# Graph attention and expert mixture: layer biases and norm shifts folded into the next projection, expert weights split two experts at a time

## The reference

```python
h = elu(layer_norm(x @ w_in + b_in, g_in, bt_in))
for i in range(3):
    identity = h
    y = gat_conv(h, src, dst, w_l[i], a_s[i], a_d[i], b_l[i])   # p = h @ w_l[i], edge softmax, sum of messages, + b_l[i]
    y = elu(y)
    y = layer_norm(y, g_l[i], bt_l[i])                          # ... * g_l + bt_l
    h = y + identity
...
# experts: softmax gates over 8 experts, three 256 x 256 products for each
h = relu(bn(x @ W1[e] + b1[e])); h = relu(bn(h @ W2[e] + b2[e])); y = h @ Wo[e] + bo[e]; out = sum_e gate_e * y_e
```

## Time and profile before

| | |
|---|---|
| median of three runs | 7070.54 us (7068.94 to 7074.64) |
| the profiled execution | 7087.27 us |
| its span, first to last instruction | 7085.5 us |
| busy: TensorE, VectorE, ScalarE, GpSimd | 5313.8, 4842.8, 4142.8, 3639.1 us |
| the three `gat_finish` stages begin at | 1451.8, 2791.2 and 4117.9 us |
| the expert stage begins at | 4270.4 us |

### The profile page before, as it was taken

How to read it: one execution, slowest core, us unless ns; L and a number is a source line. 1 busy time by engine, 2 the same in 40 slices (tenths; PEclk the granted TensorE clock), 3 DMA queues, 4 the chain that set the end, 5 groups by cost and what they waited for, 6 DMA issues and landing times. The chain is left out here.

```text
span 7085.5 us, 94548 instructions
## 1 busy us (share of the span) xinstructions
PE 5313.8 (75%) x22314; PEld 3799.3 (54%) x22314; DVE 4842.8 (68%) x13222; ACT 4142.8 (58%) x13411; POOL 3639.1 (51%) x3571
## 2 busy tenths in 40 slices
PE   1768888745888886668888616999989787877688
PEld 1645555333555554545555315888874566655346
DVE  5656666694777777767777596666662677778673
ACT  4578888874898988579889762333336322111132
POOL 3477777737777773577777700000000577777201
PEclk8878888876999998779999767999999898887789
DMA  6444444344444443444444332000007534333302
GB/s 184 124 123 116 117 118 117 106 132 139 119 121 122 121 118 104 131 138 124 118 122 118 109 108 65 19 18 27 19 23 267 166 116 128 109 107 101 105 17 74
DMA packets 484001, 763.77 MB, mean 108 GB/s; under 512 B 85543, under 2 KB 360695, under 8 KB 483511
## 3 DMA queue, kind: packets, MB, share of 16 engines
q0 software_dynamic: 166320, 446.82, 22.7%
q1 hardware_dynamic: 317335, 313.36, 13.9%
HBM read 622.82 MB, written 146.27 MB: 109 GB/s over the span
## 5 line engine op out<-in xcount | busy, mean ns | idle before, releaser
L1806 POOL DMA_INDIRECT gm_got<-scratch_feat,keep_src_tab x2490 | 2500.6, 1004 | 776.0 <-issue 669.6
L2028 ACT ACTIVATE gm_got<-gm_got 128x64 f32<-128x64 f32 x9828 | 2393.6, 335 | 5.8 <-DVE gm_got L1941 5.8
L2083 PE MATMUL gm_bank<-gm_got,gm_onehot 128*128 128x264 f32 x4980 | 1783.1, 466 | 385.9 <-DVE gat_acc L1966 229.4
L2083 PEld LDWEIGHTS gm_bank<-gm_got,gm_onehot 128*128 128x128 f32 x4980 | 938.4, 217 | 897.8 <-DVE gat_acc L1966 370.1
L1966 DVE TENSOR_TENSOR gat_acc<-gat_acc,gm_bank 128x264 f32 x2490 | 1059.1, 425 | 498.8 <-PE gm_bank L2083 231.5
L1114 POOL DMA_INDIRECT mix1a_got<-scratch_rel_feat,layer_rel_tab x240 | 240.4, 1002 | 1529.2 <-issue 1528.0
L1114 POOL DMA_INDIRECT mix1b_got<-scratch_rel_feat,layer_rel_tab x590 | 586.9, 995 | 190.5 <-issue 187.2
L1171 PE MATMUL mix1b_m_bank<-mix1b_got,mix1b_onehot 128*128 128x256 f32 x1180 | 379.6, 459 | 153.6 <-DVE layer_acc L1145 132.1
L837 POOL DMA_INDIRECT scratch_first<-gat_scores,keep_first_pos x150 | 216.5, 1444 | 466.9 <-DVE gat_scores L820 425.7
L1973 DVE TENSOR_TENSOR gm_onehot<-keep_iota_row,keep_dst_tab 128x896 f32<-128x896 f32 x357 | 386.5, 1083 | 25.8 <-PE gm_bank L2083 21.9
L1171 PEld LDWEIGHTS mix1b_m_bank<-mix1b_got,mix1b_onehot 128*128 128x128 f32 x1180 | 245.7, 225 | 253.3 <-DVE mix1b_onehot L1123 166.4
(11 more groups left out here) (558 smaller groups left out, 10760.2 us busy)
## 6 DMA issues: line engine op xcount, KB each, us to landing
scratch_rel_feat<-rel_out SPq DMA_DIRECT2D x50, 1024.0 KB, 6.3
gm_got<-scratch_feat,keep_src_tab POOLq DMA_INDIRECT x2490, 2.8
gm_flags<-scratch_flags SPq DMA_DIRECT2D x90, 280.0 KB
gf_feat<-scratch_feat SPq DMA_DIRECT2D x75, 256.0 KB, 4.4
gf_old<-scratch_hidden SPq DMA_DIRECT2D x75, 256.0 KB, 4.7
scratch_hidden<-gf_h SPq DMA_DIRECT2D x75, 256.0 KB, 4.0
scratch_feat<-gf_row SPq DMA_DIRECT2D x50, 260.0 KB, 3.3
gm_x<-scratch_x SPq DMA_DIRECT2D x50, 256.0 KB, 3.1
```

Of the source, the lines that this page charges most:

```text
L1806: nc.gpsimd.indirect_dma_start(out=got[:, place // GROUPS, place % GROUPS * GROUP + j, 0:GAT_ROW], out_offset=None, in_=dram["feat"][layer ...
L2028: last = nc.scalar.activation(rows, rows, ACT.Copy, scale=got[:, b, i, D + h:D + h + 1])
L2083: nc.tensor.matmul(bank[i % BANKS][:, 0:GAT_SUM], onehot[:, i % HOTS, :], got[:, v[1] % B, i, :], start=True, stop=True).then_inc(s_sum, 1)
```

## The change

In the GAT stages the shift `bt_l` is no longer added to the rows. `finish_onto` writes `h = data * rstd + old` in one instruction per tile, instead of `finish` and a sum. What is missing from `h` is a constant row, the sum of the `bt_l` so far. The next projection puts it back: at the start of the stage the constant row is multiplied with `w_l` and added to `b_l` of the coming layer, giving `shift` (its first row filled, the rest zero), and each tile's projection gets one more matmul, of a matrix whose first row alone is ones (`first_row`) with `shift`, accumulated in PSUM. The attention scores get their part from `sc_shift` in the sums that replace two copies. As the attention weights sum to one, `b_l` can go through the projection too, and the sum L2237 goes in layers 1 and 2 (counted from 0; layer 0 keeps it). The expert stage adds the three `bt_l` to its rows.

In the expert stage the first node rows and the weights of experts 0 and 1 are loaded first; the parameters come after; the cutting is done by groups of two experts, the high parts on ScalarE; the rest of the groups is loaded and cut inside the first unit, which stands unrolled ahead of the loop.

```diff
@@ GroupNorm
+    def finish_onto(self, nc, p, out, data, base):
+        u = p % UNROLL
+        nc.vector.wait_ge(self.s_centred, p + 1)
+        for i in range(PAIR):
+            last = nc.vector.scalar_tensor_tensor(out[:, i, :], data[:, i, :], self.rstd[:, u, i:i + 1], base[:, i, :], ALU.mult, ALU.add)
+        return last
@@ Projection.start_sp (layer > 0)
+                for i in range(self.layer):
+                    sp.dma_start(self.c_col[:, i, :], self.io["L0_gnn_bt_l"][i].rearrange("(a p) -> p a", p=P)).then_inc(self.s_c, 16)
+            sp.dma_start(self.b_row[:, :], self.io["L0_gnn_b_l"][self.layer].unsqueeze(0)).then_inc(self.s_c, 16)
@@ Projection.start_dve (layer > 0)
+        nc.vector.memset(self.shift[:, :], 0.0)
+        nc.vector.tensor_copy(self.first_row[:, :], self.ident[:, 0:1].to_broadcast([P, P])).then_inc(self.s_col, 1)
...
+        dve.wait_ge(self.s_line, 1)
+        nc.vector.tensor_tensor(self.shift[0:1, 0:D], self.score_bank[0:1, 0:D], self.b_row[:, :], ALU.add)
+        nc.vector.tensor_copy(self.shift[0:1, D:], self.score_bank[0:1, D:D + 2 * GAT_HEADS]).then_inc(self.s_shift, 1)
+        dve.wait_ge(self.s_spread, 1)
+        nc.vector.tensor_copy(self.sc_shift[:, :], self.score_bank[:, 0:2 * GAT_HEADS]).then_inc(self.s_lined, 1)
@@ Projection.start_pe (layer > 0)
+        for out, rhs in ((self.score_bank[0:1, 0:D], self.w), (self.score_bank[0:1, D:D + S], self.wa)):
+            for k in range(HALVES):
+                last = mm(out, self.c_col[:, 0, k:k + 1], rhs[:, k, :], start=(k == 0), stop=(k == HALVES - 1))
+        last.then_inc(self.s_line, 1)
+        pe.wait_ge(self.s_shift, 1)
+        mm(self.score_bank[:, 0:S], self.first_row[:, :], self.shift[:, D:], start=True, stop=True).then_inc(self.s_spread, 1)
@@ Projection.project_pe
-        project_pair(self.nc, bank, self.ht[:, u], self.w)
+        if self.layer:
+            for i in range(PAIR):
+                out = bank[:, i * D:(i + 1) * D]
+                for k in range(HALVES):
+                    self.nc.tensor.matmul(out, self.ht[:, u, k, i * P:(i + 1) * P], self.w[:, k, :], start=(k == 0), stop=False)
+                self.nc.tensor.matmul(out, self.first_row[:, :], self.shift[:, 0:D], start=False, stop=True)
@@ Projection.scores_dve (layer > 0): two sums with sc_shift in place of two copies
+            self.nc.vector.tensor_tensor(row, sc[:, :, 0:GAT_HEADS], add[:, :, 0:GAT_HEADS].to_broadcast([P, tiles, GAT_HEADS]), ALU.add)
+            self.nc.vector.tensor_tensor(scores, sc, add.to_broadcast([P, tiles, 2 * GAT_HEADS]), ALU.add).then_inc(self.s_sc, size)
@@ gat_finish, vector engine
-                        elif name == "finish":
-                            ln.finish(nc, p, yp, rows["bt_l"]).then_inc(s_ya, 1)
...
-                            nc.vector.tensor_tensor(h[:, u], old[:, p % DEEP], yp, ALU.add).then_inc(s_h, 1)
+                            ln.finish_onto(nc, p, h[:, u], yp, old[:, p % DEEP]).then_inc(s_h, 1)
...
-                        if name == "sums":
+                        if name == "sums" and not layer:
                             dve.wait_ge(s_yf, p + 1)
                             nc.vector.tensor_tensor(yp, yp, both(rows["b_l"][:, :]), ALU.add).then_inc(s_yb, 1)
@@ expert_mixture, sync engine
+                load(sp, 0, slice(0, QUAD))
+                for to, frm in shifts:
+                    sp.dma_start(to, frm).then_inc(s_shift, 16)
+                for j in range(3):
+                    load_weight(j, 0)
                 (the 13 small loads)
-                for j, (to, frm) in enumerate(w_loads):
-                    if j == 2:
-                        sp.wait_ge(s_cutw, 1)
-                    sp.dma_start(to, frm).then_inc(s_wj[j], 16)
-                sp.wait_ge(s_cutw, 2)
-                for s in range(2):
-                    load(sp, s, slice(s * QUAD, (s + 1) * QUAD))
+                for j in range(3):
+                    load_weight(j, 1)
+                load_weight(0, 2)
+                load_weight(1, 2)
+                for j in (1, 2):
+                    sp.wait_ge(s_cutw[j], 2)
+                load(sp, 1, slice(QUAD, 2 * QUAD))
+                load_weight(2, 2)
+                for j in range(3):
+                    load_weight(j, 3)
@@ expert_mixture, front_start
                     c.done(nc.vector.tensor_tensor(x[:, s], x[:, s], h[:, s], ALU.add))
+                    c.done(nc.vector.tensor_tensor(x[:, s], x[:, s], after_gat[:, :].unsqueeze(1).to_broadcast([P, QUAD, D]), ALU.add))
@@ expert_mixture, vector engine
-                for j in range(3):
-                    (wait, high part and low part of a whole tensor)
+                front_start(0, 32)
+                front_statistics(0)
+                front_end(1, 0)
+                cut_weights(0, 0)
                 cut_rows(1)
+                parameters()
+                for j in (1, 2):
+                    cut_weights(j, 0)
+                unit(1, 0, 0, 32, cutting=True)
@@ expert_mixture, scalar engine: the high parts, in the first unit by group_due(e)
+                def high_weights(j, g):
+                    act.wait_ge(s_wg[j][g], 16)
+                    nc.scalar.copy(w_high[j][:, experts(g), :, :], whole(j, g)).then_inc(s_high[j], 1)
```

More of the change, by code:

```diff
@@ L756, in __init__ @@
         self.s_sent = space.sems("p_sent", UNROLL)
+        if layer:
+            self.c_col = sb("c_col", [P, layer, HALVES])
+            self.b_row = sb("b_row", [1, D])
+            self.first_row = sb("first_row", [P, P])
+            self.shift = sb("shift", [P, D + 2 * GAT_HEADS])
+            self.sc_shift = sb("sc_shift", [P, 2 * GAT_HEADS])
+            self.s_c, self.s_col, self.s_line, self.s_shift, self.s_spread, self.s_lined = (
+                sem(f"p_{n}") for n in ("c", "col", "line", "shift", "spread", "lined"))
         self.first, self.first_pos = dram["first"], keep["first_pos"]
@@ L2118, in gat_finish @@
         sb, sem = space.sb, space.sem
-        rows = {n: sb(n, [P, D]) for n in ("b_l", "g_l", "bt_l")}
+        rows = {n: sb(n, [P, D]) for n in (("g_l",) if layer else ("b_l", "g_l"))}
         feat, old, y = (sb(n, [P, DEEP, PAIR, D]) for n in ("feat", "old", "y"))
@@ L3218, in gather_expert, with unit @@
                         dve.sem_inc(s_done, 1)
-                def unit(n, s, m, next_loaded, size=QUAD):
+                def unit(n, s, m, next_loaded, size=QUAD, cutting=False):
                     gates(n, s, size)
@@ L3287, in layer, with unit @@
                     last.then_inc((s_h1, s_h2)[j], 1)
-                def unit(n, s, m, last, size=QUAD):
+                def unit(n, s, m, last, size=QUAD, cutting=False):
                     act.wait_ge(s_logit, n)
@@ L3297, in unit @@
                         if e >= 1:
+                            if cutting and e == 2:
+                                act.wait_ge(s_cutw[2], 1)
                             layer(1, m + e, e - 1, size)
@@ L3300, in unit @@
                             front_root(n + 1)
+                        if cutting:
+                            for j, g in group_due(e):
+                                high_weights(j, g)
+                high_weights(0, 0)
                 front_root(1)
                 turned(1)
-                with act.Fori(0, N_U // 2) as r:
-                    for s in range(2):
-                        unit(r * 2 + s + 1, s, r * (2 * E) + s * E, False)
+                for j in (1, 2):
+                    high_weights(j, 0)
+                act.wait_ge(s_var, 1)
+                nc.scalar.activation(shift[:, :, :], par[:, :, 4, :], ACT.Sqrt, bias=bn_eps[:, 0:1]).then_inc(s_root, 1)
+                act.wait_ge(s_scale, 1)
+                unit(1, 0, 0, False, cutting=True)
+                with act.Fori(0, N_U // 2 - 1) as r:
+                    for s in (1, 0):
+                        k = 2 - s
+                        unit(r * 2 + k + 1, s, r * (2 * E) + k * E, False)
+                unit(N_U - 1, 1, (N_U - 2) * E, False)
                 unit(N_U, 0, (N_U - 1) * E, True, REST)
@@ L3310, in _ @@
             def _(pe):
-                pe.wait_ge(s_w, 16 * len(loads))
-                for j in range(2):
-                    for i in range(5):
-                        last = nc.tensor.transpose(bank1[j][:, 16 * i:16 * i + 16], par_rows[:, j, i, :], keep["ident"][0:16, 0:16])
-                    last.then_inc(s_par, 1)
-                pe.wait_ge(s_scale, 1)
                 def turn(n, s):
@@ L3336, in wide, with unit @@
                     return last
-                def unit(n, s, m, last_unit, size=QUAD):
+                def unit(n, s, m, last_unit, size=QUAD, cutting=False):
                     pe.wait_ge(s_xtc, n)
@@ L3371, in unit @@
                             pe.wait_ge(s_acc, m + (e - 1))
+                            if cutting:
+                                pe.wait_ge(s_cutw[2], (e - 2) // AT_ONCE + 1)
                             for i in range(size):
```

(16 more changed lines are left out.)

137 lines of the change are left out of this document (95 added, 42 removed).

## The result

The changed kernel takes 7052.09 us (median of 9 runs, 7043.26 to 7057.63) where the kernel before takes 7074.64 on the same chip (9 runs, 7068.94 to 7081.69): ratio 0.9965, 95% interval [0.9955, 0.9974]. On another chip the same pair gave 0.9968 [0.9954, 0.9981]. The time fell by 22.5 us, 0.32%; the forecast was -10.5 us. The profiled execution took 7043.26 us, its span 7041.5.

What follows compares the result with a forecast made beforehand. VectorE was taken to bound the third closing stage, TensorE the end of the first two and the expert units. -28.5 + 23 + 17 - 22 = -10.5 us gave 7060 us, range 7048 to 7074, with rivals 7038 to 7080.

Steps and rivals of the forecast that it cites:

- The third closing stage, -28.5: Third GAT layer's closing stage, bound by VectorE: two sums a pair go, 30.1 us, about 1.4 comes back; -28.5 us.
- The start-up, 4.7 us bare: Ahead of the first burst in the first two closing stages: `start_dve`'s round trip with TensorE, 4.7 us, covered by nothing.
- The loop from scores to scores: First two closing stages: ScalarE's copies, scaling and root, then TensorE's burst, 34 us a step; +18.4 and +16.5 us.
- I take 4.0 and a burst of 21.6 us: TensorE's projection of five pairs: 17.6 us at full clock plus 4.0 for the low clock at its start.
- short ramps: Rival: all ten TensorE bursts have a short low-clock part, 2 us less each; -31 in all, 7040 us; chance 0.17.
- bursts of 19 or of 26 us (clock): Sign that the forecast is wrong: five-pair bursts in the first two closing stages last this long instead of about 21.6 us.
- level in the middle: First two closing stages: TensorE's projection is level with VectorE in their middle and sets their end; waits 1.91, 10.13, 6.33 us.
- The experts' terms 17.7, 2.7 and 3.4: Expert stage's start: rows until cut 17.7 us, parameters 2.7, TensorE's routing 3.4; first product after 24 us instead of 48.9.
- The clock stays low: Rival: bursts run at 1.2 GHz for 16 instead of 8 us, 4 us more each; +29 in all, 7100 us; chance 0.06.
- The experts, -22: Expert stage: first product 24.7 us earlier, 2 us charged for cutting inside the first unit; -22 us.
- A stalled first unit: Rival: late loads or cuts and the parameters cost half the experts' head start, 12 us; +2 in all, 7072 us; chance 0.15.
- The additional sum of the other fronts: Shift sum in the other 11 expert fronts: falls into a 1.18 us wait, costs 0.1 each; without that cover 13 us.

Runs made afterwards that it cites:

- row_thin: The changed kernel with the additional matmul on only the first partition of both operands, still float32; 7256.88 us, ratio 1.0253 to the kernel before the change.
- row_cut: The changed kernel with the row added by two fp32r passes, each from one partition, in place of two of float32; 7208.36 us, ratio 1.0182.
- experts_only: The kernel before the change with only the reordered start of the expert stage, GAT stages as they were; ratio 0.9970 to the kernel before.
- after_again: The changed kernel run once more, unchanged, on another chip beside a version with a one-pass row; ratio 0.9968 to the kernel before.
- after: The changed kernel itself; 7052.09 us, ratio 0.9965 to the kernel before the change.
- before: The kernel without the change; 7074.64 us on the chip of the main comparison.
- no_row: The changed kernel without the additional matmul, so the projected rows lack the shift; ratio 0.9942 to the kernel before the change.
- shift_first: The changed kernel with the three broadcast shift rows loaded ahead of the node rows in the expert stage; 7060.16 us, ratio 0.9968.

## Why the prediction came out as it did

The forecast left the direction open, and its sum was 12 us short of the medians. The median lies inside the forecast's own range, but in part by luck: the two closing stages that it took to lose 40 us lost 17.5, and had the medians followed the -33.9 of the touched stages, they would have come to 7037 us, below both of its ranges. By its own steps:

- *The third closing stage, -28.5*: right, -28.7, with VectorE still the bound (busy 112.7 of the stage's 123.8 us, and from 18.4 us after its start on without a wait of over 0.5 us). The ten other kernels with the edit have 123.4 to 124.4 us.
- *The start-up, 4.7 us bare*: 3.9 and 4.1, right. But the experiments say that it isn't the term to save: laid ahead of the sums, it delays ScalarE's list, which then sets the first burst only 0.6 us earlier.
- *The loop from scores to scores*: the place was right, and so was ScalarE's 12.4 us. The step that was mis-sized is the burst, "I take 4.0 and a burst of 21.6 us". It measured 19.0 to 20.4, because **the low-clock part is no constant of the pause before it; it fell from 4.0 to 2.2 us when the burst got the additional matmuls**. Steps of 31.7, 29.8, 27.2, 17.8 and 8.4 us came in place of 34, 31.4, 28.6, 20.2 and 8.4 in the first closing stage (114.9 for 122.7), and 114.4 in the second. So +10.6 and +8.2 us there, +3.3 and -2.3 at the first scores where +5.6 and +1.0 were said, and -1.1 each behind the last where it was -0.8. This is the rival "short ramps", to which 0.17 was given: what spoke for it was taken for chance (two bursts of ten), and that the work in the burst would be changed by the edit itself was not asked. The forecast's own sign "bursts of 19 or of 26 us (clock)" came true on its low side.
- *Two slips in its working*: the 1.91 us is the wait of the second group, and the waits of the third and fourth, 3.36 and 9.26, are left out of "level in the middle". The experts' terms 17.7, 2.7 and 3.4 add up to 23.8 us, which is 25.1 earlier than before and not 24.7. Neither would move the sum by more than 0.4.
- *The same rule seen from the skill*: the Trainium skill (TensorE: Matmul & The Clock Gate, What's actually happening) calls the slow start short and dependent on phase. The changed kernel's bursts, 1.6 to 3.0 us extra, come nearer to that; those of before, 4.2 to 4.7 in eight of ten, do not agree with it.
- *The clock stays low*: it did not, but `row_thin` and `row_cut` show that this rival was near. With the zeros left out of the operands, as one might to save work, it would have come, at 75 to 102 us a stage above the changed kernel.
- *The experts, -22*: -22.7 in this pair of traces and 24 by the ratio of `experts_only` (11 to 35), so right as far as that can be told, with two errors against each other. The first product came 21.0 us sooner and not 24.7, since the first sum waited 3.8 us longer, for the broadcast shift rows; the first unit lasted 2.0 us longer (80.7 us from its first logits to the next unit's, 78.7 before), as charged. The rest of the units made up the difference in this trace, by some 3.6 us, within what the stage varies. A stalled first unit is ruled out. The additional sum of the other fronts does not show: the later units last 76.5 to 79.6 us, 76.4 to 79.7 before.
- *What stays open*: -33.9 us in the touched stages against -22.5 (interval -32 to -18) in the medians, and -30 in those of `after_again`. The untouched stretches and the expert stage vary by more than the difference, and no run isolates them. Open too is why the row brought the rise of the clock forward.

## What to carry to other kernels

When a matmul is added to a short burst after idleness, size the burst with and without it, since where the clock rises is part of the price, and it can move either way. A constant row can be added to a product in PSUM for 0.12 us a tile with one fp32r pass, high and low part in two partitions and zeros in the rest; keep the operand over all 128 partitions. And when a bare wait is to be hidden by moving work, first read which engine waits for what stands behind the new place: here it was ScalarE, and of 4 us of waiting 0.6 were gained.

## What the runs showed of the hardware

- A two-pass float32 matmul of 128 by 256 in PSUM accumulation takes 0.43 us with its row in one partition and zeros in the other 127, at 2.4 GHz (`after`, L847). Cut to one partition it keeps TensorE at 1.2 GHz through whole stages (`row_thin`: 0.52 over 260 us with TensorE busy for 224; `after`: 0.83 over 160 us with TensorE busy for 113), and takes 1.15 us, where the full one takes 0.86 at that clock. One-partition passes of fp32r did the same (`row_cut`: 0.50 with TensorE busy all of 30 us).
- Eight of ten bursts without the row stay at 1.2 GHz for some 9 us (twice the extra of the table; `before`, `no_row`), all bursts with the full row for some 3 to 6, after the same pauses of 4 to 10 us.
- Three rows of 1 KB, each broadcast to 128 partitions, were usable 8.8 us after their issue behind 1 MB of node rows (`after`), and 5.6 us when issued first (`shift_first`).
